# Attention in a four-layer kernel: when the row transfers start, and in how many parts expert 0 is loaded and split

## The reference, cut to what matters

```
x = x + attn(layernorm(x))          # 16 heads of 16, softmax over 512 keys
x = x + ffn(layernorm(x))           # top 2 of 8 experts, w1: 256 x 704, w2: 352 x 256
x = x + mamba(layernorm(x))
x = x + moe(layernorm(x))
```

## Time and profile before

| | |
|---|---|
| time, median of 3 runs | 2366.66 us (2366.48 to 2369.31) |
| the profiled execution, its own time | 2365.99 us |
| its span in the trace | 2363.8 us |
| busy shares | PE 82%, PEld 48%, DVE 73%, ACT 51%, POOL 61% |
| attention phase | the slots end at about 674 us, the serial tail at about 745 us |

### The profile page before, as it was taken

The page is one execution under the profiler, slowest core; times in us unless marked ns, Lnnn a source line. Parts: engine busy times, 40 slices in busy tenths (PEclk is TensorE's granted clock), DMA queues, the critical chain, the costliest instruction groups (busy, mean ns, idle before and its releaser), DMA issues. The chain is left out here.

```text
span 2363.8 us, 32538 instructions
## 1 busy us (share of the span) xinstructions
PE 1949.9 (82%) x9782; PEld 1140.1 (48%) x9782; DVE 1720.0 (73%) x2430; ACT 1199.2 (51%) x2459; POOL 1434.5 (61%) x1165
## 2 busy tenths in 40 slices
PE   2599999998864999917889898989898977659998
PEld 1244444443334999914334344434343433247776
DVE  4488878885645555522999999999999999755654
ACT  1066666675633333315675767575757565222222
POOL 7334444533342444412999999999999999533444
PEclk9599989998866999958999998989898998968999
DMA  3545445452143444423040404040304040011100
GB/s 81 102 105 107 98 105 115 103 125 93 46 145 110 74 77 77 62 49 147 15 144 18 144 18 144 18 143 18 143 18 143 9 144 9 17 48 36 36 31 23
DMA packets 231200, 185.57 MB, mean 79 GB/s; under 512 B 148713, under 2 KB 201585, under 8 KB 231042
## 3 DMA queue, kind: packets, MB, share of 16 engines
q1 hardware_dynamic: 216162, 162.61, 24.2%
q0 software_dynamic: 13296, 17.77, 4.3%
q10 hardware_dynamic: 1584, 3.24, 0.4%
HBM read 134.07 MB, written 49.49 MB: 78 GB/s over the span
## 5 line engine op out<-in xcount | busy, mean ns | idle before, releaser
L1682 POOL TENSOR_TENSOR mb_dbu<-mb_dtu,mb_bbc 128x1024 f32<-128x1024 f32 x256 | 601.3, 2360 | 69.5 <-DVE mb_hp L1824 45.2
L1887 PE MATMUL mb_y_ps<-mb_hc,mb_ident 128*128 128x512 f32 x640 | 328.5, 639 | 77.7 <-DVE mb_hc L1832 77.7
L463 ACT ACTIVATE ex_plain<-at_t_ps 128x512 f32<-128x512 f32 x512 | 289.8, 595 | 199.7 <-PE at_t_ps L839 189.7
L1826 DVE TENSOR_TENSOR_SCAN mb_da_ps<-mb_da_ps,mb_dbu 128x1024 f32<-128x1024 f32 x160 | 365.2, 2283 | 17.2 <-ACT mb_da_ps L1735 17.2
L598 DVE TENSOR_REDUCE at_mx<-at_s_ps 128x2 f32<-128x1024 f32 x256 | 310.8, 1219 | 51.8 <-PE at_s_ps L848 50.0
L848 PE MATMUL at_s_ps<-ex_w 48*128 48x512 f32 x512 | 229.9, 513 | 36.1 <-DVE at_mx L598 21.6
L1887 PEld LDWEIGHTS mb_y_ps<-mb_hc,mb_ident 128*128 128x128 f32 x640 | 123.3, 202 | 245.2 <-issue 124.5
L839 PE MATMUL at_t_ps<-ex_w 64*128 64x512 f32 x512 | 222.8, 491 | 16.1 <-ACT ex_plain L463 10.7
L1688 POOL TENSOR_TENSOR mb_hp<-mb_hp,mb_cbc 128x1024 f32<-128x1024 f32 x96 | 226.5, 2360 | 0.0
L1824 DVE TENSOR_TENSOR_SCAN mb_hp<-mb_da_ps,mb_dbu 128x1024 f32<-128x1024 f32 x96 | 218.8, 2279 | 0.0
L1121 POOL DMA_INDIRECT x<-m_o,m_xs x71 | 113.6, 1601 | 169.7 <-DMA x<-m_o,m_xs 99.8
(11 more groups left out here) (315 smaller groups left out, 4118.5 us busy)
## 6 DMA issues: line engine op xcount, KB each, us to landing
mb_bbc<-mb_scr SPq DMA_DIRECT2D x64, 512.0 KB, 5.9
mb_cbc<-mb_scr SPq DMA_DIRECT2D x64, 512.0 KB, 4.8
ex_w<-at_scr SPq DMA_DIRECT2D x384, 64.0 KB, 2.3
m_xs<-rt_rows SPq DMA_DIRECT2D x71, 129.0 KB
at_scr<-at_qk_hi SPq DMA_DIRECT2D x32, 256.0 KB
at_scr<-at_qk_lo SPq DMA_DIRECT2D x32, 256.0 KB
at_xin<-in_x SPq DMA_DIRECT2D x32, 128.0 KB, 2.2
ex_plain<-in_x SPq DMA_DIRECT2D x8, 512.0 KB
```

What stands on the lines that cost most here:

```text
L463: act.activation(probs[:, c, h, :], t_ps[:, k % 2, :], ACT.Exp, scale=SCALE).then_inc(exp_done, 1)
L1682: pool.tensor_tensor(dbu[:, q % 3, :, :], dtu_2, bbc[:, 2 * p:2 * p + 2, :], ALU.mult).then_inc(S["dbu_ready"], 1)
L1826: dve.tensor_tensor_scan(da, da, add, 0.0, ALU.mult, ALU.add).then_inc(S["scan_done"], 1)
L1887: last = pe.matmul(y_ps[:, v % 2, :], ident[:, :], src[:, j, :], start=(q == tile_first[v] and j == 0), stop=(q == tile_last[v] and j == 1))
```

## The change

Three edits. Before each `scatter` of the loop, POOL waits for `v_ps_ready` of its slot, that is for the last matrix product of `project_values` in it. The upper halves of experts 0 and 1 are copied in four pieces of 544 columns, spread over steps of slots 27 and 31, where two pieces of 1088 followed each other after step 1. Expert 0's three loads are issued in slots 24, 25 and 26, one in each; POOL's subtraction for expert 0 moves from the end of slot 27 to the end of slot 28.

```diff
-    def upper_parts(self, act, k):
-        act.wait_ge(self.loaded[k], 48)
-        for hi, lo, raw in self.pieces(k):
-            last = act.activation(hi, raw, ACT.Copy)
-        last.then_inc(self.hi_done, 1)
+    def piece(self, k, i, n):
+        a, b = i * HALF // n, (i + 1) * HALF // n
+        return self.w[:, k, a:b], self.w[:, k, HALF + a:HALF + b], self.plain[k][:, 0, HALF + a:HALF + b]
+    def upper_piece(self, act, k, i, n):
+        if i == 0:
+            act.wait_ge(self.loaded[k], 48)
+        hi, lo, raw = self.piece(k, i, n)
+        ins = act.activation(hi, raw, ACT.Copy)
+        if i == n - 1:
+            ins.then_inc(self.hi_done, 1)
...
-                    if t == 25:
+                    if 24 <= t < 27:
                         sp.wait_ge(qk_ps_ready, 4 * NB)
                         sp.wait_ge(xT_ps_ready, NT)
-                        experts.load(sp, A, 0)
+                        experts.load(sp, A, 0, slice(t - 24, t - 23))
...
                         if (n := batch(t, 13 + c)) is not None:
+                            pool.wait_ge(v_ps_ready, min(t + 3, NT))
                             scatter(n, c)
-                    if t == 27:
+                    if t == 28:
                         experts.lower_parts(pool, 0)
...
-                        if t in (27, 31) and k == 1:
-                            experts.upper_parts(act, (t - 27) // 4)
+                        if t == 27 and k in (2, 6, 12, 14):
+                            experts.upper_piece(act, 0, (2, 6, 12, 14).index(k), 4)
+                        if t == NT - 1 and k in (2, 4, 6, 10):
+                            experts.upper_piece(act, 1, (2, 4, 6, 10).index(k), 4)
```

More of the change, by code:

```diff
@@ L92, in carve, with load @@
         return flat.rearrange(f"p ({' '.join(names)}) -> p {' '.join(names)}", **dict(zip(names, shape[1:])))
-    def load(self, eng, A, k):
+    def load(self, eng, A, k, parts=slice(0, 3)):
         raw = self.plain[k][:, 0, HALF:2 * HALF]
-        for dst, src in ((raw[:, 0:W1].rearrange("p (k f) -> p k f", k=2), A["m0_w1"][k].rearrange("(k c) f -> c k f", k=2)),
-                         (raw[:, W1:W1 + 2 * D], A["m0_w2a"][k]),
-                         (raw[0:F0 - 2 * P, W1 + 2 * D:HALF], A["m0_w2"][k, 2 * P:F0, :])):
+        every = ((raw[:, 0:W1].rearrange("p (k f) -> p k f", k=2), A["m0_w1"][k].rearrange("(k c) f -> c k f", k=2)),
+                 (raw[:, W1:W1 + 2 * D], A["m0_w2a"][k]),
+                 (raw[0:F0 - 2 * P, W1 + 2 * D:HALF], A["m0_w2"][k, 2 * P:F0, :]))
+        for dst, src in every[parts]:
             eng.dma_start(dst, src).then_inc(self.loaded[k], 16)
-    def pieces(self, k):
-        for a, b in ((0, HALF // 2), (HALF // 2, HALF)):
-            yield self.w[:, k, a:b], self.w[:, k, HALF + a:HALF + b], self.plain[k][:, 0, HALF + a:HALF + b]
+    def piece(self, k, i, n):
[8 more added lines that the diff above has]
+            ins.then_inc(self.hi_done, 1)
     def upper_parts(self, act, k):
-        act.wait_ge(self.loaded[k], 48)
-        for hi, lo, raw in self.pieces(k):
-            last = act.activation(hi, raw, ACT.Copy)
-        last.then_inc(self.hi_done, 1)
+        for i in range(2):
+            self.upper_piece(act, k, i, 2)
     def lower_parts(self, eng, k):
         eng.wait_ge(self.hi_done, k + 1)
-        for hi, lo, raw in self.pieces(k):
+        for i in range(2):
+            hi, lo, raw = self.piece(k, i, 2)
             last = eng.tensor_tensor(lo, raw, hi, ALU.subtract)
```

## The result

The changed kernel takes 2345.45 us, median of 4 runs (2341.81 to 2348.05), beside 2366.57 us (2365.67 to 2369.31) of the kernel before: a ratio of 0.9908, with a 95% interval from 0.9891 to 0.9925. That is 21 us less, 2.6 us beyond the forecast of 2348.0 and inside its range. The profiled execution took 2341.81 us, with a span of 2339.7. It is the shortest of the four, so the two traces differ by 24.2 us where the medians differ by 21.1.

What follows compares the result with a forecast made beforehand. The chained engines PE, ACT, DVE and POOL bound the attention slots, stalled in three. Gains 3.1 + 8.2 + 2.9 + 2.5 + 3.0 - 1.0 = 18.7 us off 2365.99, plus 0.67 for the median, gave 2348.0 us; range 2338 to 2358.5.

Steps and rivals of the forecast that it cites:

- The stall: Slots 25, 26, 29: row-transfer issues during the value projection hold PE's signals; removal gains 3.1, 8.2 and 2.9 us.
- the lock: Slot 29: POOL's moved subtraction holds DVE's small routing steps through the shared port pair; loss 1.0 us, between 0 and 2.5.
- The signs named for it: Slots 25, 26, 29: no remote wait at L756; first transfer issue more than 0.4 us after the projection's last product.
- PE works on: Slot 25: PE keeps working during the transfer issues while DVE and ACT sit still for 4.9 and 5.1 us.
- Slot 27: Slot 27: clock mostly returns once stall and copy block go; gain 2.5 us, between 0 and 3.0.
- The sign that was named for this: Slot 27 still at clock 0.74 would mean that the narrow products alone lower the clock.
- The copies: Slot 31: copying in four pieces removes PE's 1.57 us wait and the low clock after; gain 3.0 us, between 0 and 7.
- The load: Slots 24 to 26: loading expert 0 in three parts changes nothing, either way.
- slower: Slots 25, 26, 29: four issues without a chunk cause the stall, so waiting only delays its end; 2373.8 us, chance 0.04.
- profile-only: Stall exists only in profiled executions, so only the copies' share, 2 us, stays; 2364.7 us, chance 0.05.
- the partial stall: Tighter slots: transfers still meet other PE work, for instance slot 26 keeps its stall; 2358.7 us, chance 0.06.
- the full return of the clock: Slots 25 to 29: clock returns altogether, all upper bounds plus about 1 us for each of four slots; 2334 us, chance 0.09.

Runs made afterwards that it cites:

- the first profile: Profiled execution of the changed kernel in its first timing, the shortest of four runs: 2341.81 us.
- the kernel with both blocks: Changed kernel with the copies of experts 0 and 1 again as two pieces of 1088 columns after step 1: 2357.17 us, ratio 0.9946.
- the kernel with plain transfers: Changed kernel plus four non-indirect POOL transfers of 128 x 256 at step 12 of slots 24, 27 and 28: 2349.64 us, one run.
- the run with two issues: Changed kernel with the first two of each batch's four transfer issues let go to meet the value projection; third chip, one run: 2341.97 us.

## Why the prediction held, point by point

**The stall.** Its place, its cause and its sum were right: slots 25, 26 and 29 give 4.0, 7.3 and 3.1 us on the second chip (predicted 3.1, 8.2 and 2.9, with 1.0 to come off the last for the lock). The signs named for it are there: no wait called remote, and the first issue of slot 25 0.84 us after the projection's end. In the first profile slot 29 gave 5.6, with slot 28 losing 1.3. In the seven other timed kernels with the wait, slots 27 to 29 take 54.1 to 54.7 us together, however they share it; the 51.4 of the profile after is the exception, and about 3 us of what that trace shows are chance. What "PE works on" missed is that the projection itself was slowed: its last products start 3.4 us after the first, where all 64 take 1.9 us. So of the wait a part was PE's work coming late, and the rest its signals.

**Slot 27, the term that failed.** I took 2.5 us for a clock that comes back. With the stall alone gone the slot takes 21.0 us at 0.76, against 19.7 at 0.74 before, so its low clock isn't a consequence of the stall. (The first profile alone would have looked like a hit, 17.8 us at 0.90.) With the pieces too it takes 17.8 to 19.9 us, but what it wins there the next two lose: slots 27 to 29 were 57.6 us together, and the 54.1 to 54.7 above are that less the 3 us of slot 29's stall. The stall and the block did go, but over the three slots that gave nothing. The sign that was named for this, a slot 27 still at 0.74, came in part: 0.76 with the wait alone and 0.83 in the changed kernel on the second chip. Why the clock falls there was not tried.

**The copies, mis-sized.** I took 3.0 us out of 0 to 7, all of it for slot 31. The sixteen transposed score products of that slot now start within 16.8 us where they took 20.6, and PE's wait of 1.57 us is gone, as was said. On the second chip the end is 97.5 and 97.6 us with pieces and 103.5 with the block, 6 us, and 7.8 us by the medians. Elsewhere it is less: 97.4 for 102.8 in the two first profiles, 99.4 for 100.7 and 103.6 on the first chip. So the wait of 1.6 us comes with every block, and the rest depends on a clock that the copies don't set alone. This and slot 27 cancel, which is luck: 5.5 us for both were written, 5 to 6 came.

**The load** is worth nothing that can be told, as written.

**The lock.** Not in the first profile: POOL's subtraction ended there at 606.23 and DVE's first step came at 606.62. In the kernel with both blocks they missed each other as well. In the ten other profiles with the subtraction in slot 28, on all three chips, they met: the step of 0.16 us takes 0.91 to 1.12 us, and 3.13 in the kernel with plain transfers, where it meets both pieces of the subtraction, beyond the 2.5 that the prediction took for the most. Slots 28 and 29 take 33.6 us together without the meeting (the first profile) and 34.7 with it (second chip), so the 1.0 is of the right size where it occurs, and it is a matter of some tenths whether it does. By the row above, where POOL's piece started first and DVE's step ended 0.03 us after it, the rule on the shared port pair (the Trainium skill, page "SBUF — State Buffer", section on its two separate sides) holds for this meeting.

**Sum.** For the slots the prediction had 14.2 + 2.5 - 1.0 = 15.7 us, and they give 14.4 on the second chip, lock included (17.7 in the first profile); for the end it had 3.0, and 5.3 came. That is 19.7 us against 18.7, with 19.9 between the medians on the second chip and 21.1 in the first timing. The one profile of the kernel before serves for all these differences, so they are good to a few microseconds. The rival "slower" fell with its own test, as no wait moved with the issues; "profile-only" fell with the timings of the kernel with the wait alone and of the kernel before beside it, 2353.83 and 2369.57 us; the partial stall fell because no slot kept its wait, and the full return of the clock because slots 24 to 28 still stand at 0.82 to 0.90.

What the prediction could not see is that its largest term isn't there on every chip. On the third one 0.0025 x 2349.68 = 5.9 us are left (3.5 to 8.2), less than the least that the sum allowed, 8.3. It is of the size of the copies' share, and leaves little for the stall. That the kernel before has no stall there is inferred from its time and from the run with two issues, since it was not profiled on that chip. And as each chip was used at one time only, the runs can't tell the chip from something else that differed then.

## What to carry over

When two engines stop together and start together, look for a third that was busy for that time, even if nothing in the program connects them, and then for the places where the same work ran without a stall: they name the condition. A block of two microseconds on an engine that others wait for can cost more than its length (here 1.6 us of waiting, and up to 7.8 us in all where TensorE's clock was lower behind it); cut in pieces it can be free. One profile shows one execution: here the first profile had slots 27 to 29 some 3 us shorter than the seven others, and no lock, which most others had. And a gain that rests on such an interference should be timed on more than one chip, and more than once, before it is put down as the kernel's.

## What was not expected of the hardware

While GpSimd issues indirect transfers of about 1 us each, a run of 64 matrix products without semaphores loses pace (the last ones in groups of four to six, one group each 0.72 to 0.76 us; undisturbed, all 64 take 1.1 us at the full clock and 1.9 us at the lower level) and TensorE's signals arrive up to 4.9 us late, until 0.9 to 1.2 us after the last of four issues. The same issues beside score products alone made no such wait (slot 22, slot 30). On two of the three chips the kernel before, without the wait, takes 2369 to 2370 us, in 12 runs or more on each; on the third it takes 2350 in 23 runs, and there a projection with an issue inside it shows no gaps and a delay of 0.25 us at most. Which resource it is was not tried.
